# The triangular inverse of all eight units together in two banks, with 512-column evictions, a bank for the transposed outputs and another order of steps

## The reference

```python
q = _causal_conv_silu(x @ w_q, conv_q)      # also k; v has 128 columns a head
q = _l2norm(q); k = _l2norm(k)
beta = sigmoid(x @ w_b) * 2.0
g = -exp(A_log) * softplus(x @ w_a + dt_bias)
def step(S, inp):                           # over the 512 tokens, per item and head
    q_t, k_t, v_t, g_t, b_t = inp
    S = S * jnp.exp(g_t)[..., None, None]
    mem = jnp.einsum('bhk,bhkv->bhv', k_t, S)
    delta = (v_t - mem) * b_t[..., None]
    S = S + jnp.einsum('bhk,bhv->bhkv', k_t, delta)
    o_t = jnp.einsum('bhk,bhkv->bhv', q_t * scale, S)
    return (S, o_t)
rms = o * lax.rsqrt(jnp.mean(o * o, axis=-1, keepdims=True) + EPS)
y = (rms * norm_w * silu(x @ w_g)) @ w_out
x = x + _layernorm(y)                       # then the experts, likewise
```

## Time and profile before

| | before |
|---|---|
| median of 3 runs | 4765.86 us |
| lowest, highest | 4765.37, 4773.78 us |
| span of the profiled execution | 4761.7 us |
| TensorE matmul, weight load | 98%, 78% busy |
| VectorE, ScalarE, GpSimd | 87%, 71%, 66% busy |
| DMA | 43 GB/s over the span |

### The profile page before, as it was taken

How to read it: one execution, slowest core, us unless ns; L and a number is a source line. 1 busy time by engine, 2 the same in 40 slices (tenths; PEclk the granted TensorE clock), 3 DMA queues, 4 the chain that set the end, 5 groups by cost and what they waited for, 6 DMA issues and landing times. The chain is left out here.

```text
span 4761.7 us, 140986 instructions
## 1 busy us (share of the span) xinstructions
PE 4665.0 (98%) x44336; PEld 3733.8 (78%) x44336; DVE 4138.2 (87%) x9914; ACT 3397.1 (71%) x10287; POOL 3152.1 (66%) x4511
## 2 busy tenths in 40 slices
PE   6999999999999999999999999999999999999798
PEld 4788888888888888888888888888888888888566
DVE  6888888888888888888888888888888889999576
ACT  5777777777777777777777777777777777777443
POOL 5666666666666666666666666666666666777565
PEclk9999999999999999999999999999999999999899
DMA  5111111111111111111111111111111111121000
GB/s 180 48 33 44 33 53 34 44 37 47 46 34 44 33 53 33 44 33 51 36 44 35 42 50 36 44 34 50 35 44 33 44 42 53 47 61 44 29 29 34
DMA packets 206732, 212.94 MB, mean 45 GB/s; under 512 B 17218, under 2 KB 180180, under 8 KB 206036
## 3 DMA queue, kind: packets, MB, share of 16 engines
q1 hardware_dynamic: 206036, 204.06, 14.0%
HBM read 186.31 MB, written 17.70 MB: 43 GB/s over the span
## 5 line engine op out<-in xcount | busy, mean ns | idle before, releaser
L1074 DVE SCALAR_TENSOR_TENSOR cv<-ps_a,wqkv,cv 128x511 f32<-128x511 f32 (+2 forms) x1536 | 1145.8, 746 | 181.6 <-ACT cv L1067 161.0
L1279 POOL TENSOR_TENSOR bm<-bat,mask 128x256 f16<-128x256 f32 x1536 | 1029.5, 691 | 0.6
L1059 PE MATMUL ps_a<-xin,wqkv 128*128 128x512 f32 x2048 | 1002.8, 612 | 3.0 <-DVE bat L1256 1.5
L1329 ACT ACTIVATE m<-b 128x256 f16<-128x256 f32 x1536 | 597.2, 389 | 376.2 <-PE b L1324 376.2
L1067 ACT ACTIVATE cv<-ps_a,wqkv 128x512 f32<-128x512 f32 x512 | 352.0, 688 | 554.3 <-PE ps_a L1059 554.1
L1340 DVE TENSOR_TENSOR tt<-tt,b 128x256 f16<-128x256 f16 x1536 | 635.4, 414 | 115.4 <-PE b L1335 114.8
L1382 ACT CAST tt<-bu 128x256 f16<-128x256 f32 x1536 | 578.2, 376 | 1.2 <-PE bu L1377 0.5
L1514 PE MATMUL ps_a<-wout,yT 128*128 128x256 f32 x2048 | 548.3, 390 | 0.5 <-ACT yT L1508 0.5
L1059 PEld LDWEIGHTS ps_a<-xin,wqkv 128*128 128x128 f32 x2048 | 349.6, 191 | 250.6 <-issue 250.6
L1207 PE MATMUL ps_b<-wgate,xin 128*128 128x256 f32 x2048 | 494.9, 384 | 0.2 <-DVE vtok L1230 0.2
L1256 DVE SCALAR_TENSOR_TENSOR bat<-ps_a,w,dec 128x256 f32<-128x256 f32 x1024 | 435.4, 477 | 40.5 <-DVE w L1126 22.4
(11 more groups left out here) (270 smaller groups left out, 12229.8 us busy)
## 6 DMA issues: line engine op xcount, KB each, us to landing
xin<-xT_scratch SPq DMA_DIRECT2D x128, 512.0 KB, 4.0
grow<-g_scratch SPq DMA_DIRECT2D x256, 256.0 KB, 4.6
gam<-g_scratch SPq DMA_DIRECT2D x256, 96.0 KB, 2.8
n_x<-in_x SPq DMA_DIRECT2D x16, 512.0 KB, 4.9
xT_scratch<-acc SPq DMA_DIRECT2D x16, 512.0 KB, 5.9
out_y<-e_yo SPq DMA_DIRECT2D x16, 512.0 KB, 2.6
gate_tok<-in_x SPq DMA_DIRECT2D x56, 128.0 KB, 2.9
wqkv<-in_w_qkv SPq DMA_DIRECT2D x32, 128.0 KB, 3.1
```

The costliest lines, as they stand in the source:

```text
L1059: ins = pe.matmul(ps[:], wqkv[:, k, j * P:(j + 1) * P], xin[p][:, k, :], start=k == 0, stop=k == KT - 1)
L1074: s.done(dve.scalar_tensor_tensor(y[:, r:], ps[:, 0:T - r], tap[:, j, TAPS - 1 - r:TAPS - r], y[:, r:], ALU.mult, ALU.add), f"a_tap{j}{r}")
L1279: s.done(pool.tensor_tensor(half_of(bm[:, l, units(g), :], l, 1), half_of(bt[:, units(g), :], l, 1), half_of(c["mask"][:, l, :].unsqueeze( ...
L1329: s.done(act.mul(half_of(m1[:, l, units(g), :], l, 0), half_bank(bank, l), -1.0), f"b_Me{l}{g}")
```

## The change

- The two halves of a level become one step of eight units: `b_M`, `b_V` and `b_U` are eight matmuls each, `b_Me`, `b_Ve`, `b_Ue` one instruction of 512 columns. `b_Tq` and `b_Tf` are joined likewise. `b_P`, `b_R`, `b_F`, `b_T` stay in halves, now in a thread `correct(g)`.
- All of it lives in two banks: `b0` (`inverse`) for `b_Tq`, `b_M`, `b_V` and the correction of half 0; `bu` for `b_U` and the correction of half 1.
- `b1` (`side`) is free for the transposed outputs: `c_yT` to `c_yTe` has a session of its own, and `co` is held from `c_O` to `c_y` only.
- `SLOT_ORDER` is another one, with some other lags.

```diff
@@ -50,26 +50,22 @@
 
 
 SLOT_ORDER = """
-    a_silu1.1 c_acc0.3 c_sq1.3 c_KS2.3 c_m1.3 b_Ue01.2 b_Me40.2 b_V40.2 b_M11.2 c_R2.3 b_Me11.2 b_U40.2 b_kT.1 c_p1.3
-    b_Ve40.2 c_Z2.3 y_turn.1 b_Ue40.2 b_sq0.1 d_ln.1 k_out.1 b_V11.2 c_y1.3 b_n0.1 b_M50.2 b_U11.2 c_u2.3 c_yT1.3
-    b_Ve11.2 y_bn0.0 y_bn1.0 b_Me50.2 b_kk0.1 b_V50.2 b_M21.2 b_Ue11.2 b_ss.1 c_yTe1.3 b_Me21.2 b_U50.2 c_SU2.3 b_rc.1
-    k_mix.1 x_mv.5 x_ve.5 c_O2.3 b_bm41.2 b_Ve50.2 b_w1.1 b_P0.2 x_rs.5 b_V21.2 b_Ue50.2 b_ev00.1 b_E1.1 b_ev01.1
-    b_kw.1 c_S2.3 d_add.1 b_Ve21.2 y_mv.0 y_ve.0 b_U21.2 a_proj2.1 d_turn.1 b_ktok.1 d_spt.1 d_beta.1 b_R0.2 c_sq2.3
-    c_m2.3 c_KS3.3 c_out1.3 d_cum.1 d_rmm.1 c_p2.3 b_M31.2 c_y2.3 y_rs.0 x_sh.5 b_Ue21.2 a_cv2.1 a_tap21.1 b_F0.2
-    c_yT2.3 x_y0.5 x_y1.5 b_diag0.1 b_vT0.2 b_t20.1 c_acc1.3 a_tap22.1 c_R3.3 y_sh.0 b_Me31.2 b_T0.2 a_tap23.1
-    d_cums.1 b_V31.2 b_gam.1 b_hi0.1 a_tanh2.1 a_proj3.1 b_Ve31.2 c_Z3.3 k_end.1 b_Tq0.1 b_bm00.1 b_vtok0.2 a_cv3.1
-    d_rows.1 c_yTe2.3 y_xT.1 y_xf0.0 b_U31.2 b_bm51.2 a_silu2.1 b_M41.2 b_Me41.2 b_Tf0.1 a_tap31.1 b_Ue31.2 b_g0.1
-    b_M00.1 c_u3.3 a_tap32.1 b_tg0.1 b_U41.2 b_V41.2 c_O3.3 b_Ue41.2 a_tap33.1 c_out2.3 b_Me00.1 b_Ve41.2 b_U00.1
-    b_sg0.1 b_M51.2 b_lo0.1 b_V00.1 a_tanh3.1 b_qT.1 a_silu3.1 c_Z0.2 c_acc2.3 c_sq3.3 b_bm10.1 b_Ve00.1 x_bn0.4
-    b_bm20.1 b_Me51.2 b_lo1.2 b_V51.2 b_kk1.1 b_Ve51.2 b_root.1 c_m3.3 c_p3.3 b_M10.1 b_Ue00.1 c_u0.2 b_sq1.1 b_U51.2
-    b_Me10.1 b_P1.2 c_y3.3 c_yT3.3 b_bm30.1 x_x0.5 x_x1.5 b_ev10.1 c_SU0.2 b_n1.1 b_ev11.1 b_Ue51.2 c_yTe3.3 y_xf1.0
-    b_V10.1 b_Ve10.1 b_U10.1 d_abs.0 d_max.0 d_exp.0 d_th.0 a_proj0 x_y2.5 x_y3.5 b_bm40.1 c_O0.2 b_diag1.1 a_cv0
-    b_M20.1 c_S0.2 b_R1.2 x_bn1.4 c_out3.3 b_Ue10.1 b_sel b_eps.1 b_Me20.1 x_x2.5 a_tap01 c_sq0.2 c_m0.2 b_gend.1
-    c_KS1.2 c_acc3.3 c_p0.2 b_vT1.1 b_E0 b_V20.1 a_tap02 b_U20.1 b_F1.2 b_T1.2 c_R1.2 a_proj1 k_turn.0 c_Z1.2 b_t21.1
-    b_bm01.1 b_bm11.1 b_kqs.1 c_ws.2 b_Ue20.1 b_Ve20.1 b_M30.1 b_Tq1.1 a_tap03 k_cp.0 k_prod.0 c_y0.2 a_tanh0 b_bm21.1
-    b_vtok1.1 c_yT0.2 a_cv1 b_Me30.1 a_silu0 b_Tf1.1 b_hi1.1 c_yTe0.2 b_g1.1 a_tap11 c_u1.2 a_tap12 b_V30.1 a_tap13
-    x_bn2.4 b_M01.1 b_Ve30.1 b_U30.1 b_tg1.1 c_SU1.2 b_sg1.1 x_bn3.4 c_O1.2 b_M40.1 b_Me01.1 b_V01.1 b_Ue30.1 b_U01.1
-    c_out0.2 b_bm31.1 c_S1.2 b_bm50.1 b_Ve01.1 x_x3.5 a_tanh1
+    c_u2.3 y_bn0 y_bn1 b_eps.2 b_vtok1.2 b_lo0.2 b_U2.2 x_mv.5 b_Ue2.2 x_ve.5 b_kT.1 b_sq0.1 b_Ve2.2 c_SU2.3 x_rs.5
+    c_acc0.3 c_y1.3 d_ln.1 b_M3.2 k_out.1 b_n0.1 b_E0.1 b_kk0.1 b_ss.1 y_mv c_O2.3 y_ve b_Me3.2 b_E1.1 b_bm41.2 b_rc.1
+    b_V3.2 c_sq2.3 b_w1.1 b_U3.2 b_ev00.1 k_mix.1 c_S2.3 b_Ve3.2 c_yT1.3 b_kqs.2 a_proj2.1 y_rs c_yTe1.3 x_sh.5
+    c_KS3.3 b_bm50.2 b_kw.1 b_Ue3.2 x_y0.5 a_cv2.1 d_add.1 x_y1.5 b_M4.2 b_ktok.1 b_Me4.2 b_root.1 b_ev01.1 d_turn.1
+    c_m2.3 y_sh b_diag0.1 d_spt.1 d_beta.1 c_out1.3 c_R3.3 a_tap21.1 b_V4.2 c_p2.3 d_cum.1 c_acc1.3 d_rmm.1 c_Z3.3
+    b_bm51.2 c_u3.3 a_proj3.1 a_tap22.1 b_gam.1 a_cv3.1 y_xT.1 b_U4.2 y_xf0 b_Ve4.2 c_y2.3 a_tap23.1 a_tap31.1 b_M5.2
+    a_tap32.1 c_yT2.3 a_tanh2.1 b_Me5.2 c_sq3.3 d_cums.1 c_O3.3 b_g0.2 b_lo1.2 b_V5.2 c_m3.3 b_Ue4.2 a_silu2.1 k_end.1
+    a_tap33.1 c_yTe2.3 b_U5.2 d_rows.1 c_out2.3 c_p3.3 b_tg0.2 x_bn0.4 c_y3.3 c_yT3.3 b_P0.2 b_Ve5.2 a_tanh3.1 b_Ue5.2
+    a_silu3.1 b_hi0.1 b_P1.2 c_acc2.3 c_yTe3.3 b_kk1.1 b_R0.2 b_R1.2 x_x0.5 b_t20.1 x_x1.5 b_diag1.1 b_sg0.2 b_t21.1
+    b_F0.2 b_ev11.1 y_xf1 b_F1.2 b_vT0.1 b_T0.2 c_Z0.2 b_ev10.1 x_y2.5 b_vtok0.1 x_y3.5 c_u0.2 c_out3.3 c_SU0.2 b_qT.1
+    b_T1.2 x_bn1.4 b_sq1.1 b_bm01.1 b_gend.1 b_bm00.1 x_x2.5 c_O0.2 c_S0.2 c_sq0.2 c_KS1.2 c_acc3.3 b_Tq.1 c_m0.2
+    c_R1.2 d_abs b_n1.1 d_max c_p0.2 d_exp b_Tf.1 d_th a_proj0 b_bm11.1 c_Z1.2 c_y0.2 b_sel b_bm21.1 a_cv0 a_tap01
+    b_M0.1 a_tap02 c_u1.2 b_bm10.1 b_Me0.1 b_bm20.1 a_proj1 c_SU1.2 a_tap03 b_V0.1 a_cv1 b_Ve0.1 b_bm30.1 b_U0.1
+    x_bn2.4 c_ws.2 c_O1.2 k_turn b_M1.1 b_Ue0.1 a_tap11 x_bn3.4 c_yT0.2 b_g1.1 a_tanh0 a_tap12 k_cp c_S1.2 k_prod
+    b_Me1.1 a_tap13 b_bm31.1 x_x3.5 c_yTe0.2 b_V1.1 c_sq1.2 b_tg1.1 b_hi1.1 b_U1.1 c_KS2.2 c_m1.2 a_tanh1 a_silu0
+    b_Ve1.1 y_turn b_sg1.1 c_out0.2 b_M2.1 c_p1.2 c_R2.2 b_Ue1.1 b_vT1.1 b_Me2.1 c_Z2.2 a_silu1 b_bm40.1 b_V2.1
 """.split()
 
...
         halves = (bank("b0"), bank("b1"))
+        inverse, side = halves
...
-            [("b_Tq0", "b_T0")], [("b_Tq1", "b_T1")],
-            [(f"b_U{l}{g}", f"b_Ue{l}{g}") for l in range(NLEV) for g in range(2)],
+            [("b_Tq", "b_T0")], [(f"b_U{l}", f"b_Ue{l}") for l in range(NLEV)] + [("b_P1", "b_T1")],
             [(f"c_KS{m}", f"c_R{m}") for m in range(1, CH)] + [(f"c_Z{m}", f"c_u{m}") for m in range(CH)]
             + [(f"c_SU{m}", f"c_S{m}") for m in range(CH - 1)],
-            [(f"c_O{m}", f"c_yTe{m}") for m in range(CH)],
+            [(f"c_O{m}", f"c_y{m}") for m in range(CH)], [(f"c_yT{m}", f"c_yTe{m}") for m in range(CH)],
...
-            for name in ("b_M", "b_Me", "b_V", "b_Ve", "b_U", "b_Ue", "b_bm"):
-                s.series(f"{name}.{g}", [f"{name}{l}{g}" for l in range(NLEV)])
+            s.series(f"b_bm.{g}", [f"b_bm{l}{g}" for l in range(NLEV)])
+        for name in ("b_M", "b_Me", "b_V", "b_Ve", "b_U", "b_Ue"):
+            s.series(name, [f"{name}{l}" for l in range(NLEV)])
...
+                return bank[:].rearrange("p (u b r) -> p u b r", u=NU, r=2 << l)
+
+            def invert():
+
+
+                if (yield "b_Tq"):
+                    s.need(pe, i, "b_t20", "b_t21")
+                    free(pe, i, "b_Tq")
+                    for u in range(NU):
+                        ins = pe.transpose(inverse[:].bitcast(F16)[:, u * P:(u + 1) * P], tt[:, 1, u, :], c["ident16"][:])
+                    s.done(ins, "b_Tq")
+                if (yield "b_Tf"):
+                    s.need(act, i, "b_Tq")
+                    s.done(act.copy(tt[:, 0], inverse[:].bitcast(F16).rearrange("p (u t) -> p u t", t=P)), "b_Tf")
                 for l in range(NLEV):
+                    even = half_of(tt[:, 0], l, 0)
+
+                    if (yield f"b_M{l}"):
+                        s.need(pe, i, f"b_bm{l}0", f"b_bm{l}1", f"b_Ve{l - 1}" if l else "b_Tf")
+                        for u in range(NU):
+                            ins = pe.matmul(half_bank(inverse, l)[:, u], bm[:, l, u, :], even[:, u], start=True, stop=True)
+                        s.done(ins, f"b_M{l}")
+                    if (yield f"b_Me{l}"):
+                        s.need(act, i, f"b_M{l}")
+                        s.done(act.mul(half_of(m1[:, l], l, 0), half_bank(inverse, l), -1.0), f"b_Me{l}")
+
+                    if (yield f"b_V{l}"):
+                        s.need(pe, i, f"b_Me{l}", *([f"b_Ue{l - 1}"] if l else ["b_t20", "b_t21"]))
+                        for u in range(NU):
+                            ins = pe.matmul(half_bank(inverse, l)[:, u], tt[:, 1, u, :], half_of(m1[:, l], l, 0)[:, u],
                                             start=True, stop=True)
+                        s.done(ins, f"b_V{l}")
+                    if (yield f"b_Ve{l}"):
+                        s.need(dve, i, f"b_V{l}")
+                        s.done(dve.tensor_tensor(even, even, half_bank(inverse, l), ALU.add), f"b_Ve{l}")
+
+            def grow_other():
+
+                for l in range(NLEV):
+                    if (yield f"b_U{l}"):
+                        s.need(pe, i, f"b_Me{l}", *([f"b_Ue{l - 1}"] if l else ["b_t20", "b_t21"]))
+                        free(pe, i, f"b_U{l}")
+                        for u in range(NU):
+                            ins = pe.matmul(half_bank(bu, l)[:, u], m1[:, l, u, :], half_of(tt[:, 1], l, 1)[:, u],
                                             start=True, stop=True)
+                        s.done(ins, f"b_U{l}")
+                    if (yield f"b_Ue{l}"):
+                        s.need(act, i, f"b_U{l}", f"b_V{l}")
+                        s.done(act.copy(half_of(tt[:, 1], l, 1), half_bank(bu, l)), f"b_Ue{l}")
+
+            def correct(g):
+
+
+                bank = (inverse, bu)[g]
                 if (yield f"b_P{g}"):
+                    s.need(pe, i, f"b_Ve{NLEV - 1}", f"b_lo{g}")
+                    if g:
+                        free(pe, i, "b_P1")
                     for k in range(4):
...
-                out, turned = co[:, 0:2 * DV], co[:, 2 * DV:4 * DV]
+                out, turned = co[:, 0:2 * DV], side[:, 0:2 * DV]
...
                 if (yield f"c_yT{m}"):
                     s.need(pe, i, f"c_y{m}")
+                    free(pe, i, f"c_yT{m}")
                     for h in range(2):
                         ins = pe.transpose(turned[:, h * P:(h + 1) * P], yy[:, h, :], c["ident"][:])
```

More of the change, by code:

```diff
@@ L1277, in masks @@
                     if (yield f"b_bm{l}{g}"):
-                        s.need(pool, i - 1, f"b_M{l}{g}")
+                        s.need(pool, i - 1, f"b_M{l}")
                         s.done(pool.tensor_tensor(half_of(bm[:, l, units(g), :], l, 1), half_of(bt[:, units(g), :], l, 1),
@@ L1342, in invert @@
+            def correct(g):
```

(25 more changed lines are left out.)

33 lines of the change are left out of this document (removed).

## The result

The changed kernel takes 4852.14 us (median of four runs, 4850.48 to 4853.03), the kernel before 4766.38 us beside it (4765.37 to 4773.78). The ratio is 1.0179, with a 95% interval from 1.0165 to 1.0194. It is slower by 86 us, where 4744 us was predicted, and above the range given (4734 to 4788).

What follows compares the result with a forecast made beforehand. TensorE's stream was taken to bound about 126 slots of 33.67 us. From 4761.7, less 25 (switches), plus 6 (waits), less 3 (drain) gave 4740, and 4.2 for the runs' median made 4744 us; range 4734 to 4788.

Steps and rivals of the forecast that it cites:

- What bounds the kernel: Middle slots: about 126 slots of 33.67 us are pure TensorE streaming; time off ScalarE or VectorE alone is worth nothing.
- The order of steps: TensorE's switches from half to full precision: 0.89 us a slot before, 0.69 after; gain 0.20 a slot, 25 us.
- Evictions: 512-column evictions on VectorE and ScalarE: less busy time, hidden behind TensorE, 0; 0.59 us on ScalarE, 0.68 on VectorE.
- New waits: TensorE waits at four closely balanced places: bounds 0 and 0.15 us a slot, taken 0.05, 6 us back.
- b_kk stands twice in each order and cancels: Switch count on TensorE: b_kk was left out as equal in both orders, so no difference.
- GpSimd* keeps its instructions: GpSimd: same instructions in both kernels, b_Tq with about 0.5 us spare for its b_t2 inputs; put at 0.
- The drain: Last item's chain after the slots: c_Z0 9.6 us into its slot, not 12.9; 3 us earlier, bounds 0 and 5.
- (a): Rival: saved switches lost to waits at the four balanced places, 4755 to 4775 us; 24% together with (c).
- (b): Rival: a strided 512-column eviction costs as two of 256; 0.40 us a slot against 0.20 saved, 4788 us; 18%.
- (c): Rival: longer distance behind half precision isn't tied to the order, no wait appears; 4763 us; 24% together with (a).
- (d): Rival: gaps in TensorE's slots bring the granted clock to 0.95, +220 us, 4965 us; 1%.

Runs made afterwards that it cites:

- 9: Kernel before with b_M31 moved ahead of c_out1 and b_M40 ahead of c_O1, adding two full-precision switches; 4855.63 us, ratio 1.0183.
- 10: Kernel before with b_M31 moved ahead of c_out1 and b_U00 ahead of c_out2, adding two full-precision switches; 4796.52 us, ratio 1.0055.
- 11: Kernel before with b_V21, b_P0, b_U21 behind c_out1 and b_F0 behind b_vT0, for one switch less; 4941.10 us, ratio 1.0360.
- Experiment 3: Changed kernel, order kept, with b_kqs multiplying only 16 of 128 columns of each block from the third item on; 4840.18 us, ratio 1.0154.
- 4: Changed kernel with the four residual statistics steps x_bn reading 8 of 256 columns; 4846.95 us, ratio 1.0158.
- 5: Changed kernel with residual steps regrouped: x_bn0 to x_bn3, x_mv, x_ve ahead of c_y0, x_rs behind b_bm31; 4823.55 us, ratio 1.0115.
- a_xrs: Changed kernel with the last items' x_rs moved behind b_kw, and x_sh, x_y0, x_y1 behind c_R3; 4848.14 us, ratio 1.0164.
- experiment 8: Changed kernel with b_E0, the decays' exponentials, moved to the end of the slot before, behind a_cv1; 4885.58 us, ratio 1.0241.
- k_sw2: Same run as 9: kernel before with b_M31 ahead of c_out1 and b_M40 ahead of c_O1; 4855.63 us, ratio 1.0183.
- k_sw3: Same run as 10: kernel before with b_M31 ahead of c_out1 and b_U00 ahead of c_out2; 4796.52 us, ratio 1.0055.
- p_less: Same run as 11: kernel before with b_V21, b_P0, b_U21 and b_F0 moved for one switch less; 4941.10 us, ratio 1.0360.
- experiment 6: Changed kernel with b_Me, b_Ve and b_Ue evicting only four of eight units, 256 columns, all matmuls kept; 4829.48 us, ratio 1.0123.
- 1: Same run as a_xrs: changed kernel with x_rs behind b_kw, and x_sh, x_y0, x_y1 behind c_R3; 4848.14 us, ratio 1.0164.
- 2: Changed kernel with the GpSimd step b_kqs moved behind b_kw, nothing else moved; 4858.52 us, ratio 1.0184.
- 7: Changed kernel with c_y3 moved behind c_acc2 on VectorE, c_yT3 behind b_kk1, c_yTe3 behind it; 4864.21 us, ratio 1.0201.
- e_bn: Same run as 5: changed kernel with x_bn, x_mv, x_ve regrouped ahead of c_y0 and x_rs behind b_bm31; 4823.55 us, ratio 1.0115.
- b_kqs: As a run, same as 2: changed kernel with the step of that name moved behind b_kw on GpSimd; 4858.52 us, ratio 1.0184.
- r_kqs2: Same run as Experiment 3: changed kernel with b_kqs cut to 16 of 128 columns from the third item on; 4840.18 us, ratio 1.0154.
- c_e0: Same run as experiment 8: changed kernel with b_E0 moved to the end of the slot before; 4885.58 us, ratio 1.0241.

## Why the prediction was wrong, step by step

**What bounds the kernel** was read rightly: TensorE's stream, where another engine's time is worth nothing by itself. The middle slot's stream is unchanged at 32.52 us.

**The order of steps: right.** Price and count of the switches are confirmed. In after, all six full-precision groups behind 64-column ones have 0.08 us, and 9 and 10 add such switches for 0.072 to 0.083 each; only 11, which was to save one, shows nothing. The 0.20 us a slot were saved.

**Evictions: right in size** (0.59, 0.68 us). The pairs for which I worked out 0.06 to 0.08 us to spare, b_M2 to b_V2 and b_M4 to b_V4, do not wait, and c_Z0 is short by the 0.05 I gave.

**New waits: the step that failed in the middle.** I took 0.05 us a slot, with 0.15 as the bound; it is 0.50. Three parts were mis-sized or missing. b_kk1: short by 0.03 in the sum, 0.12 measured, 0.09 too little. b_kT: I had followed the inverse's banks and VectorE's stretch, but not the sessions of the shared bank `ps_b`, where b_vtok1 must end before b_kT starts; 0.12, absent from the sum. c_O2 behind b_kk0: "b_kk stands twice in each order and cancels" held for the b_kk and not for what comes behind one; 0.10. The remaining 0.16 are small ones (c_Z0, a_proj3, c_yT1). 110 slots make +31 us where -17 was the sum's share (110 x (0.05 - 0.20)).

**The last slots: missing altogether.** I followed only steps that every slot has. The x_ steps run in eleven full slots only, at new neighbours, and cost 3.2 us in each. Experiment 3 finds 1.05 us in b_kqs meeting nk, 4 finds 0.7 in the statistics on VectorE; 5 recovers 2.3 with both. The distances place the 0.9 that 5 leaves: 0.37 at a_proj2, where nk still meets the end of b_kqs, 0.39 between c_out1 and b_V4, and 0.21 between c_KS1 and b_Tq. Of the second the profile of after shows the reason. ScalarE, then TensorE:

```profile
4279.81 0.59 ACT L980 ACTIVATE acc<-acc,x_shift,x_rstd 128x256 f32<-128x256 f32 x1
```

```profile
4280.94 0.41 PE L1326 MATMUL b<-m,tt 128*128 128x64 f16 x8 [0.23 <-ACT m L1321]
```

The scaling x_y1 stands in front of b_Me4 on ScalarE, and b_V4 waits for b_Me4. In front of b_t21 on GpSimd an add, x_x0, stands likewise, and b_Tq waits for b_t21; neither was tested by a run. What failed is the term "*GpSimd* keeps its instructions", put at 0: the instructions are the same, and the time at which one runs sets what it does to VectorE.

**The first slots: missing altogether.** +15.7 us, of which some 6 can be the variation of two starts. That a_proj3 has nothing behind it, since steps of the same item moved apart, is read from the trace, not tested: a kernel that puts those steps back was not run. The lower clock makes some 3.7 us of it (45.2 against 41.5 in a_xrs with the same waits). What the first wait, for b_E0, is worth experiment 8 leaves open.

**The drain: wrong.** -3 us was forecast and +1.2 came, which is no more than the drains of before's order vary (391.0 to 394.6 us in before, k_sw2, k_sw3 and p_less). The last c_Z0 of after, in TensorE's timeline, against the earlier trace rows:

```profile
4511.49 0.71 PE L1414 MATMUL cs<-vtok,tinv 128*128 128x128 f32 x4
```

It comes 54.4 us behind the last b_kT (4457.12), not 46.6 as before. I had set it 9.6 us into its slot by the chain's own length; but the steps keep their places in the list, and in this list c_Z0 stands near the middle of the slot.

**The rivals.** (a), waits eat the saving, has the right mechanism and only half the size. (b) has the right sign, but its cause is only a part: with shorter evictions (experiment 6) 23 us come back. (c) falls with the measured switches. (d) did not come: the clock is 1.00 in the slots, so TensorE's gaps of 0.4% in the middle and 6% in the last slots did not lower it; only in the first slots, with waits of 5 us, did it fall. The clause there that a single chain in one bank would be dangerous does not follow from a rule on cycling through banks, and the new kernel cycles through them too.

In one sum: 4761.7 + 15.7 + 31 + 40 + 1.2 = 4849.6 against a profiled span of 4849.2 us.

## What to carry to other kernels

A stream on one full engine can be priced to hundredths of a microsecond from start-to-start distances. A new order is not judged by that price: every step's inputs and bank must be followed, shared banks first. A balance near nil decides nothing: b_kk1, short by 0.03 in the sum, waited 0.12, and b_V2, with 0.06 to spare, did not wait. Price the slots that are not typical as well, the first ones with their missing stages and the last with their extra steps; here they held 56 of 87.5 us. Where VectorE and GpSimd work side by side, look at what one runs while the other does; a step that comes late or early can lie over another for the first time. And taking a wait away by moving a step tends to bring the next engine's limit: of the six reorderings here that were to gain (1, 2, 5, 7, 8, 11), only number 5, which moved work into an idle stretch seen in the trace, gained more than the measurement can tell.

## What was not expected of the hardware

- A VectorE tensor_scalar on eight columns takes 0.17 us alone and 1.47 us beside a GpSimd tensor_tensor of 1.81 us; a tensor_tensor on a single element 0.14 and 1.18. It ends when the other does: nk 0.03 us after b_kqs in after and e_bn (1.47 and 0.40 us), and 0.03 us after b_bm50 in the runs b_kqs, r_kqs2 and c_e0 (0.32, 0.67 and 0.58 us). In the middle slots of after, where nothing lies over nk, it has 0.17.
- A wait in front of a half-precision group can cost more than its length when full precision follows: in k_sw2 0.19 us of wait and 0.22 more to the next start. It does not always: in k_sw3 0.08 of wait in front of b_U00 and nothing but the switch behind it, in the last slots of after 0.39 in front of b_V4 and nothing more. Why was not tested.
- Full-precision matmuls behind the b_kk (64 rows of operands) cost 0.10 us, more than behind 64-column half precision (0.08).
